# A new order for the first five images of a one-core edge, attention and sign-weight kernel

## What is computed

```python
def tok(x, scharr):                     # x: 16 x 3 x 256 x 256, uniform in 0..1
    gray = einsum('bchw,c->bhw', x, (0.2989, 0.587, 0.114))[:, None]
    edges = conv_general_dilated(gray, scharr, (1, 1), 'SAME')      # two 3x3 filters
    return abs(edges).sum(axis=1) / 2                                # 16 x 256 x 256
def attn(x):                            # 16 heads of 16, D_C = 64
    c_q = x @ W_dq;  Q = c_q @ W_uq
    c_kv = x @ W_dkv;  K = c_kv @ W_uk;  V = c_kv @ W_uv
    scores = where(causal, Q K^T / 4, -inf);  return softmax(scores) V @ W_o
h = tok(x)
h = h + attn(layernorm(h))
h = h + layernorm(h) @ sign(weight).T
```

## Time and profile before

| | us |
|---|---|
| median of three runs | 435.75 (434.21 to 435.9) |
| the profiled execution | 436.89 |
| its span, first to last instruction | 435.10 |
| TensorE busy (matmul) | 368.5 (85%) |
| VectorE, ScalarE, GpSimd busy | 288.9, 238.9, 172.0 |

### The profile page before, as it was taken

How to read it: one execution, slowest core, us unless ns; L and a number is a source line. 1 busy time by engine, 2 the same in 40 slices (tenths; PEclk the granted TensorE clock), 3 DMA queues, 4 the chain that set the end, 5 groups by cost and what they waited for, 6 DMA issues and landing times.

```text
span 435.1 us, 9881 instructions
## 1 busy us (share of the span) xinstructions
PE 368.5 (85%) x3545; PEld 261.5 (60%) x3588; DVE 288.9 (66%) x539; ACT 238.9 (55%) x408; POOL 172.0 (40%) x367
## 2 busy tenths in 40 slices
PE   0335686999999999999999999999999989796764
PEld 0122364666676767676767676767676757574442
DVE  2224176886868687868686868686878776775520
ACT  2123425666767676767676767676757563534301
POOL 7032022545554546454545454545434323212200
PEclk9998669799999999999999999999999989898975
DMA  5966797959596878787878787675753534200000
GB/s 173 226 157 149 181 257 203 269 171 257 174 245 187 230 209 220 208 223 202 219 202 223 202 224 201 199 210 160 203 151 102 145 108 132 88 27 1 26 24 24
DMA packets 72266, 74.13 MB, mean 170 GB/s; under 512 B 6387, under 2 KB 66075, under 8 KB 72219
## 3 DMA queue, kind: packets, MB, share of 16 engines
q1 hardware_dynamic: 71355, 73.11, 61.5%
q10 hardware_dynamic: 864, 0.39, 0.3%
HBM read 51.98 MB, written 21.04 MB: 168 GB/s over the span
## 4 chain that ended last, share of the span: by engine, by line
PE 75%; DMA 7%; issue 5%; ACT 5%; DVE 4%; SPq 1%; POOL 1%; ACTq 0%; POOLq 0%
PE bank L910 14%; PE bank L1034 8%; PE bank L971 7%; PE bank L921 7%; PE bank L998 6%; PE bank L947 4%; PE bank L937 4%; PE bank L903 4%; PE bank L956 3%; PE bank L973 3%; PE bank L1037 3%; PE bank L1000 3%; PE bank L1015 3%; PE bank L984 3%; DMA q_st<-top_rows 3%
## 5 line engine op out<-in xcount | busy, mean ns | idle before, releaser
L628 ACT ACTIVATE probs<-bank 128x1024 f32<-128x1024 f32 x64 | 65.2, 1018 | 50.9 <-PE bank L1000 50.2
L774 DVE TENSOR_REDUCE top<-bank 128x4 f32<-128x1024 f32 x64 | 78.0, 1219 | 19.6 <-PE bank L973 19.5
L784 DVE TENSOR_TENSOR bank<-bank,cap_kq 128x512 f32<-128x512 f32 x64 | 44.7, 698 | 23.0 <-PE bank L1015 21.6
L971 PE MATMUL bank<-k_st,q_st 96*128 96x256 bf16 x256 | 48.3, 283 | 2.8 <-DMA k_st<-qk_parts 2.8
L921 PE MATMUL bank<-rows,band 102*32 102x256 f32 x512 | 34.1, 411 | 17.4 <-DMA rows<-gray_padded 17.4
L998 PE MATMUL bank<-q_st,k_st 99*128 99x256 bf16 x256 | 47.3, 278 | 1.0 <-DMA q_st<-top_rows 0.8
L1034 PE MATMUL bank<-probs,v_ring 128*32 128x256 f32 x512 | 42.4, 403 | 3.9 <-DVE rest L761 1.9
L779 DVE TENSOR_REDUCE top<-bank 128x4 f32<-128x512 f32 x64 | 41.6, 649 | 0.0
L471 POOL TENSOR_SCALAR var<-mv 128x2 f32<-128x2 f32 x16 | 3.6, 227 | 95.2 <-DVE mv L816 95.2
L633 ACT ACTIVATE probs<-bank 128x512 f32<-128x512 f32 x64 | 38.0, 594 | 3.8 <-DVE bank L784 3.6
L791 DVE STREAM_TRANSPOSE u<-bank 128x256 f32<-128x256 f32 x64 | 28.7, 448 | 11.1 <-PE bank L1037 5.9
(11 more groups left out here) (97 smaller groups left out, 750.9 us busy)
## 6 DMA issues: line engine op xcount, KB each, us to landing
x_sb<-in_x SPq DMA_DIRECT2D x16, 768.0 KB, 6.0
rows<-gray_padded SPq DMA_DIRECT2D x48, 256.0 KB
qk_parts<-parts SPq DMA_DIRECT2D x48, 256.0 KB, 3.1
q_st<-qk_parts SPq DMA_DIRECT2D x96, 128.0 KB, 3.0
k_st<-qk_parts SPq DMA_DIRECT2D x96, 128.0 KB, 3.0
gray_padded<-gray SPq DMA_DIRECT2D x16, 258.0 KB, 3.1
out_dram<-z SPq DMA_DIRECT2D x16, 256.0 KB, 3.0
rows<-gray_padded SPq DMA_DIRECT2D x32, 24.0 KB
```

What stands on the lines that cost most here:

```text
L628: nc.scalar.activation(probs[:, g, :, 0:S], ps_k0, ACT.Exp, scale=SCALE).then_inc(exp0_done, 1)
L774: nc.vector.tensor_reduce(top[:, 1, g // 2, :, g % 2], ps_hi, AX.X, ALU.max, negate=True).then_inc(max_hi_done, 1)
L784: nc.vector.tensor_tensor(ps_k1, ps_k1, cap_kq[:, :].unsqueeze(1).to_broadcast([P, G, P]), ALU.min).then_inc(capped, 1)
L971: nc.tensor.matmul(ps_hi[:, i, :], q[:, hh, P:S], k[:, hh, :], start=(i == b * two), stop=False, skip_group_check=True)
```

## The change

It reorders the work of images 0 to 4 and leaves the rest of the pipeline as it is, apart from one place in SP's list.

- SP: the projection weights and the ones go to ScalarE's DMA queue. In the lead-in, image 3's gray is stored ahead of image 0's parts, its rows are loaded after image 0's operands, and image 2's rows stand between the two halves of these. Image 1's parts and operands are moved by SP ahead of image 4's and 5's pixels. `load_operands` waits for the third part only before the last two of six loads. In turn 1, `store_gray(4)` and `load_rows(4)` stand among image 2's parts and ahead of its operands. In every turn the pixel load comes after the operand loads, not before.
- Layer norm of images 0 and 1: sum, statistics, variance and shift on VectorE by halves (`sum_and_scale`); only the power stays on GpSimd (`root_x`).
- Parts of images 0 and 1 are cut by halves, key half first.
- TensorE: `filters(2)`, with its own banks `ps_edge2`, goes from turn -1 into turn 0; `turn_x(2)`, `compress(2)`, `expand_qk(2)` go from turn 0 into turn 1; the turn of the weight's signs, with VectorE's making and copying of them, goes from turn 1 to turn 2. `turn_max(0, 0)` comes earlier in its turn.

The diff, cut:

```diff
+        ps_edge2 = bank[:, 3:5, :].rearrange("p t (f w) -> p t f w", f=FILTERS)
@@ SP
             def load_operands(n, hf):
                 sp.wait_ge(parts_out[n % 2], 2 * 16 * (n // 2 + 1))
-                sp.wait_ge(third_out[n % 2], 16 * (n // 2 + 1))
                 need(sp, k1_done, NG * (n - ST_RING + 1))
                 for j in range(len(FROM_Q)):
+                    if j == 2:
+                        sp.wait_ge(third_out[n % 2], 16 * (n // 2 + 1))
...
-                if i >= 0:
-                    if live(i + 1):
-                        store_parts(i + 1)
-                        store_third(i + 1)
...
-                    elif live(i + 5):
-                        load_x(i + 5)
-                    if live(i + 1):
-                        load_operands(i + 1, 0)
-                        load_operands(i + 1, 1)
...
+            load_operands(1, 1)
+            load_x(4)
+            load_x(5)
+            load_outputs()
+            for i in range(1, LAST + 1):
+                if live(i + 1):
+                    store_parts(i + 1)
+                if i == 1:
+                    store_gray(4)
+                if live(i + 1):
+                    store_third(i + 1)
+                if i == 1:
+                    load_rows(4)
+                if live(i + 1):
+                    load_operands(i + 1, 0)
+                    load_operands(i + 1, 1)
+                if live(i + 5):
+                    load_x(i + 5)
+                if live(i + 4):
+                    store_gray(i + 4)
...
@@ GpSimd
+            def root_x(n):
+                pool.wait_ge(var_done, n + 1)
+                pool.tensor_tensor(rstd[:, :], var[:, :], power[:, :], ALU.pow).then_inc(rstd_done, 1)
...
+            for n in range(ON_VECTOR):
+                root_x(n)
@@ ScalarE
+            def second_part_halves(n):
+                for k, i in enumerate((1, 0)):
+                    act.wait_ge(rest_done, 2 * n + k + 1)
+                    nc.scalar.copy(parts[:, n % 2, 1 + 4 * i, :, :], rest[:, i, :, :]
+                                   ).then_inc(part1_done if k else key_part1_done, 1)
...
+            first_gray(0)
+            first_gray(1)
+            load_projections()
+            set_ones()
+            both_edges(0)
+            normalize_x(0)
+            first_gray(2)
+            copy_xt(0)
+            copy_c(0)
+            first_gray(3)
+            first_part(0)
+            second_part_halves(0)
+            both_edges(1)
+            copy_v(0)
+            normalize_x(1)
+            copy_xt(1)
+            copy_c(1)
+            first_part(1)
+            second_part_halves(1)
...
+                if i == 1:
+                    first_part(2)
+                    first_gray(4)
+                    second_part(2)
+                    copy_v(2)
+                    normalize_x(3)
@@ VectorE
+            def sum_and_scale(n):
+                for t in range(T):
+                    dve.wait_ge(abs_done, T * n + t + 1)
+                    nc.vector.tensor_tensor(h_ring[:, n % H_RING, t, :], edge[:, t, 0, :], edge[:, t, 1, :],
+                                            ALU.add).then_inc(h_done if t else top_h_done, 1)
+                    dve.wait_ge(h_done if t else top_h_done, n + 1)
+                    nc.vector.bn_stats(stats[:, t, :], h_ring[:, n % H_RING, t, :]).then_inc(stats_done, 1)
...
+                nc.vector.tensor_scalar(var[:, :], mv[:, :, 1], EPS, None, ALU.add).then_inc(var_done, 1)
+                dve.wait_ge(rstd_done, n + 1)
+                nc.vector.scalar_tensor_tensor(shift[:, :], mv[:, :, 0], -1.0, rstd[:, :],
+                                               ALU.mult, ALU.mult).then_inc(shift_done, 1)
+            def third_part_halves(n):
+                for k, i in enumerate((1, 0)):
+                    dve.wait_ge(part1_done if k else key_part1_done, n + 1)
+                    nc.vector.tensor_tensor(parts[:, n % 2, 2 + i, :, :], rest[:, i, :, :],
+                                            parts[:, n % 2, 1 + 4 * i, :, :], ALU.subtract
+                                            ).then_inc(part2_done if k else key_part2_done, 1)
@@ TensorE
                 if live(i - 1):
                     key_scores_first(i - 1, 0)
                     key_scores_second(i - 1, 0)
+                if i == 1:
+                    turn_x(2)
...
+                if i == 0:
+                    expand_v(1)
+                    filters(2)
+                    turn_max(0, 0)
...
-                if i == 1:
-                    pe.wait_ge(signed, 1)
-                    pe.wait_ge(v_copied, 3)
-                    turn(ps_w, signs, turned)
...
+                if i == 2:
+                    pe.wait_ge(signed, 1)
+                    pe.wait_ge(v_copied, 4)
+                    turn(ps_w, signs, turned)
...
-                if live(i + 3):
+                if live(i + 3) and i != -1:
                     filters(i + 3)
```

More of the change, by code:

```diff
@@ L61 @@
 ON_VECTOR = 2
+BY_SCALAR = 5
 def live(n):
@@ L1026, in values @@
                     need(pe, yt_copied, upto(n - 2))
+                if g == 0 and n == 0:
+                    pe.wait_ge(rest_done, 2 * 3)
                 if g == 1:
-                    need(pe, xt_copied, upto(n + 3))
+                    need(pe, xt_copied, upto(n + 3) if n else 3)
                 if g == 2:
@@ L1088, in _ @@
                     turn_y(i - 3)
+                if i == 1:
+                    compress(2)
                 if live(i - 1):
                     turn_max(i - 1, 1)
-                if live(i + 1):
+                if live(i + 1) and i not in (0, 1):
                     expand_v(i + 1)
```

215 lines of the change are left out of this document (116 added, 99 removed).

## The result

The changed kernel takes 448.44 us (median of four runs, 446.66 to 451.27), beside 435.82 us for the kernel before: ratio 1.029, 95% interval 1.024 to 1.033. It is slower, outside the forecast range. The profiled execution took 446.89 us, its span is 445.1, 10.0 us more than before. Medians and ranges in this document are over all executions; ratios leave out the few that ran over 1.5% above the fastest of the same kernel.

The account below looks back on a forecast made before the run. From 93.10 us on TensorE's own work was taken to set the end, so gains lay ahead of it. -5.2 + 1.8 - 0.4 = -3.8 us, against the median 435.75, gave 431.95, say 432.0; range 428.0 to 436.5.

Parts of the forecast that it names:

- the -0.4 us for the moved pixel load: Steady turns: image load behind operand reads takes some of 1.0 us; -0.4, bounds -1 and +1.
- if that cover went, ... each turn would lengthen: SP's round in the steady turns: without its idle time the next image's operands come late; no size given.
- the steady turns left 21.7: Sign against the forecast: steady turns no longer taking 21.7 us.
- part 1: Lead-in: projection weights and ones move to ScalarE's queue; taken as 0, bounds -1 and +2 us, first filters at 17.4.
- Parts 2 and 3: Lead-in: LN on VectorE gains 2.4 us, parts cut in halves gain 2.9; image 0's stores start at 34.3.
- Part 4: Lead-in, SP's new order: image 0's first score comes 10 us earlier than 55.92, by 46.0.
- its last term: End of turn 1: SP binds, image 2's operands land late; one more us on 23.0, from 86.9 to 87.9.
- the 5.2 us: Gain up to turn 2, which was to begin in effect at 87.9 instead of 93.10.
- 1.8 (bounds 0.6 to 4.0): Turn 2's cost for the moved signs: 0.60 us on TensorE and 1.2 through VectorE.
- A: Rival, turns 0 and 1: full clock through turn 0, turn 1's waits overlap; 427.5 us, chance 0.15.
- B: Rival, turn 1: image 2's serial chain, through DMA, costs what the lead-in gave; 435.0 us, chance 0.20.
- C: Rival, turn 1: image 4's pixels land late and everything waits; a 6.3 us wait gives 438.2 us, chance 0.10.

Follow-up runs that it names:

- experiment 1: The changed kernel with the pixel load ahead of the operand loads again in every turn; 442.62 us, ratio 1.014.
- experiment 5: The changed kernel with the pixel load ahead of the operand loads from turn 2 on, behind them in turn 1 only; 438.92 us, ratio 1.008.
- 12: The changed kernel with the gray store put between the operand loads and the pixel load; 443.08 us, ratio 1.016.
- 2: The kernel before with only the pixel load moved behind the operand loads, from turn 1 on; 451.69 us, ratio 1.036.
- experiment 6: experiment 5 with the weights and the ones issued by SP at their old places; 434.46 us, ratio 0.997.
- 9 to 11: experiment 5 with image 2's pixels loaded behind image 1's rows; then also weights on SP; then also image 4's VectorE gray sooner; 438.64, 438.18, 435.44 us.
- 3: experiment 1 with the weights and the ones issued by SP at their old places; 442.24 us, ratio 1.012.
- 13: experiment 6 with VectorE's gray of image 4 moved right behind the remainders of image 2's parts; 434.03 us, ratio 0.992.
- 14: 13 with the pixel load behind the operand reads and the gray store in every turn; 439.46 us, ratio 1.008.
- 4: The changed kernel with the pixel load last in SP's round, behind the gray store and the rows; 449.4 us, ratio 1.027.

## Why the prediction was wrong, point by point

**The step that failed** is the -0.4 us for the moved pixel load, with "SP's own round has idle time in the steady turns, so I cost the moved load there at nothing". From the start of turn 3 to image 15's filters it measured +8.5 us. The idle time was there, 3.2 us a round, but I did not hold it against what the move would do to the landings. I had counted issue time and asked whether the pixels would come late for their user. The cost lay elsewhere, with the small store issued right behind them, for which SP waits while everything else queues behind SP. Of the 10.0 us of span, 8.9 were lost between the start of turn 4 and image 15's filters, on top of 0.6 won before, and 1.7 are the clock of the tail; experiment 1 gives 5.8 us back though it loses 4 in turn 2, experiment 5 gives 9.5 back, 12 cures the steady turns by exchanging two lines, and 2 makes the loss alone, at 15 us. This is shown. It is not the whole miss: with the steady turns cured, experiment 5 still takes 438.92 us, above the range's 436.5. With part 1 undone too (experiment 6, 434.46) the time comes into the range. The prediction did name the fault as its condition ("if that cover went, ... each turn would lengthen"; "I would be wrong if ... the steady turns left 21.7"), but gave it no chance and no price, and none of the rivals was it.

**Part 1, weights and ones on ScalarE's queue**: taken as 0, bounds -1 and +2. The first filters came at 20.23, not 17.36: +2.87, outside the bounds. The rows were issued at 10.76, 0.4 later than before, and took longer. Summed from the GB/s of stretches of up to three us, the DMA engines moved about 2.29 MB from 9 us to the first filter instead of 1.56, and the 0.73 MB between them, at the 228 GB/s of the earlier trace rows, are 3.2 us. Image 2's 768 KB of pixels were issued at 13.59 instead of 15.90, before the rows had landed. In other kernels with this order the first filters start at 19.0 to 20.9, so the loss is 1.6 to 3.5 us. With the pixels moved they start at 18.0 to 18.25 (9 to 11), with weights, ones and pixels all as before at 17.2 to 17.7 (3, 6, 13, 14). So the pixels are a part of it; how the rest divides between weights, ones and chance is not shown, though the loss by all three together is. I had counted the pixels as "sooner" and charged nothing for it. The Trainium skill's statement that queues of different engines share the same 16 DMA engines (DMA: Bandwidth & Descriptors, Issuing engines are not separate DMA queues) agrees, and it speaks for a loss here rather than for the zero I took.

**Parts 2 and 3 were right.** Timeline of image 0 in the changed kernel, as the earlier trace rows:

```profile
20.23 3.64 PE L998 MATMUL bank<-rows,band 102*32 102x256 f32 x32 [20.23 <-DMA rows<-gray_padded]
...
26.98 1.09 ACT L599 ACTIVATE xn<-h_ring,shift,rstd 128x256 f32<-128x256 f32 x2 [2.45 <-DVE shift L821]
...
34.72 1.07 ACT L617 CAST parts<-bank 128x512 bf16<-128x512 f32 x2 [1.73 <-PE bank L1024]
...
37.30 1.51 SPq L317 DMA_DIRECT2D qk_parts<-parts  x3
...
48.49 0.61 PE L1048 MATMUL bank<-k_st,q_st 96*128 96x256 bf16 x2
```

The gap of LN is 2.45 us (forecast 2.4), from the first cast to the store 2.58 (2.5). Part 4 holds too: the first score is at 48.49, 2.5 us behind the forecast, with the filters 2.9 late. With part 1 undone, experiment 6 stores at 34.38 (34.3) and scores at 45.81 (46.0).

**Turns 0 and 1 were each forecast a little too short.** Turn 0: 17.9 us forecast, 18.8 measured, half clock in filters(2) as said. Turn 1: 24.0 with its last term, 24.88 measured. The stall of 3.93 us is gone, but the V product waited 1.54 for remainders where I had 0.9, and TensorE waited 1.52 for image 4's rows. Start and length in turn 1: the V product's wait, then GpSimd's third part, VectorE's gray beside it, the gray store, the rows, and the first operand read.

```profile
76.39 0.64 PE L1115 MATMUL bank<-probs,v_ring 128*32 128x256 f32 x8 [1.54 <-DVE rest L835]
...
77.40 2.13 POOL L477 TENSOR_TENSOR parts<-rest,parts 128x1024 bf16<-128x1024 f32 x1 [1.64 <-ACT parts L627]
...
78.26 1.82 DVE L792 SCALAR_TENSOR_TENSOR gray<-x_sb,gray 128x512 f32<-128x512 f32 x1
...
80.83 0.36 SPq L297 DMA_DIRECT2D gray_padded<-gray  x1
...
83.68 1.31 SPq L307 DMA_DIRECT2D rows<-gray_padded  x3
...
85.73 0.55 SPq L337 DMA_DIRECT2D q_st<-qk_parts  x1
```

Image 4's gray is stored at 80.83, not 76.8, and the operands are read from 85.73, not 82. The 92.17 for turn 2 are thus 87.9 plus 2.5 (first score), 0.9 (turn 0) and 0.9 (turn 1). Even with part 1 undone (experiment 6) it began at 90.7: of the 5.2 us only 2.4 exist, since in that run the first turned score came at 65.73, not 63.9, and turn 1 took 25.0.

**Turn 2 paid less than I took**: 21.23 us, 0.74 over before, where I had 1.8 (bounds 0.6 to 4.0). Away from GpSimd's third part, the first pass of the signs takes 0.38 us, where I had 0.28 or, at the worst, 2.08:

```profile
101.32 0.38 DVE L780 TENSOR_SCALAR above<-raw_w 128x512 f32<-128x512 f32 x1
```

It was 2.08 in the earlier trace rows. The gray pass at 78.26 now lies there instead and takes 1.82 where it takes 0.69 alone, ending 0.55 after GpSimd's. Both are what the Trainium skill says of the shared port pair (SBUF — State Buffer, Who interferes with whom).

**The rivals.** A: the clock fell to half in turn 0, so no. B: its extra wait for the rows of image 4 is there (1.52 us) and turn 1 is the longer for it, but that is not what made the result. C: image 4's pixels did not hold up turn 1, so that the slower time is not C's. That late pixels are dear through ScalarE's list was right in kind, and it was seen in experiments 4 and 14.

## What to carry to other kernels

Where one engine issues all transfers in order and waits for their landings, price a moved load by the landings of what is issued right behind it, then hold that growth against the round's slack, which is the time that the issuer waits for engines and not for transfers. A short store that others wait for goes ahead of a large load, not behind it: exchanging two lines gave 5.4 us here. A landing may also grow where the slack covers it: in experiment 1 the gray store, 8.4 us behind the pixels, mostly took 4.5 to 5.4 us instead of 3.1, and the turns stayed at 21.7. And an early load is not free in a lead-in either, as it can take the bandwidth of the one that is waited for.

## What the runs showed of the hardware

- A store of 258 KB issued 0.6 us behind a load of 768 KB on the same queue took 6.2 us to land (median); 8.2 to 8.8 us behind it mostly 4.5 to 5.4 (experiments 1 and 3), 9.8 to 13 us behind it 2.9 to 4.3 (the kernel before), and 3.7 when issued just ahead of it (median, experiment 12). The load took 5.2 to 7.5 (medians). The rows that wait for the store are issued as it lands, and these times are counted to there where no median is named.
- After nearly the same work TensorE's speed differs between two executions: experiments 6 and 13 have their first scores at 45.81 and 45.95, but the second filters of turn 0 took 1.93 us in 6 and 3.64 in 13, and the first turned scores are at 65.73 and 67.30. Repeated runs of one kernel spread over 430 to 437 us (experiment 13). Behind image 15's filters the profiled executions take 103.9 to 107.4 us for the same work, with mean granted clocks of 0.89 (experiment 13, 104.0), 0.88 (before, 105.5) and 0.86 (after, 107.2); whether this makes the spread of one kernel too was not tested.
- In experiment 6 the granted clock stands at 1.00 for turn 0 in the records while the filters of 54.72 took 3.64 us. In experiment 13, where the record gives 0.50 for the same filters, they took 3.64 too. The record of the clock can thus miss a fall, and the matmuls' own time is the surer sign.
